# A transformer block with experts on one Trainium2 core: new beats of the first stage and a new order within the slots of the second attention

## The reference

```python
x = x + xattn0(layernorm(x), ctx)   # 16 heads of 8: cross attention, then self attention, then a Gelu FFN of 512,
                                    # each with projection, residual and layer norm
x = x + ffn0(layernorm(x))          # router top-2 of 8 experts with capacity (SiLU, inner 512) + shared expert (SiLU, 1024)
x = x + xattn1(layernorm(x), ctx)   # one head of 128, both directions, linear interpolation 77 -> 128, sigmoid gate
x = x + ffn1(layernorm(x))          # 8 experts, each takes its 33 best tokens of 128; h = gelu(tokens @ w1 + b1) @ w2 + b2
```

## Time and profile before

| | us |
|---|---|
| median of 3 runs | 1101.03 |
| lowest, highest | 1100.28, 1107.3 |
| the profiled execution | 1104.57 |
| its span in the profile | 1102.8 |
| eight beats without an FFN in it, starts of `s2` at 105.40 and 124.45 | 19.05 |

### The profile page before, as it was taken

How to read it: one execution, slowest core, us unless ns; L and a number is a source line. 1 busy time by engine, 2 the same in 40 slices (tenths; PEclk the granted TensorE clock), 3 DMA queues, 4 the chain that set the end, 5 groups by cost and what they waited for, 6 DMA issues and landing times.

```text
span 1102.8 us, 23340 instructions
## 1 busy us (share of the span) xinstructions
PE 978.3 (89%) x8694; PEld 766.7 (70%) x8694; DVE 651.8 (59%) x2135; ACT 585.8 (53%) x1341; POOL 466.7 (42%) x752
## 2 busy tenths in 40 slices
PE   4888898988888789899989999979978998989998
PEld 2556665656566567788878887857766876778877
DVE  4658865767576864756763333657786466455331
ACT  4668887786767677423333332333334653654453
POOL 6236645658585845666620000234455245113010
PEclk8889998897989899999999999988999998998999
DMA  7745442323232202000011332300001332321421
GB/s 182 184 122 152 113 118 69 85 64 84 82 82 77 76 18 83 13 14 6 4 37 53 106 105 56 105 20 20 20 20 18 99 87 25 82 77 38 137 61 55
DMA packets 72944, 78.58 MB, mean 71 GB/s; under 512 B 8469, under 2 KB 64132, under 8 KB 72832
## 3 DMA queue, kind: packets, MB, share of 16 engines
q1 hardware_dynamic: 67104, 69.61, 22.9%
q0 software_dynamic: 4096, 6.84, 2.9%
q10 hardware_dynamic: 1632, 0.64, 0.3%
HBM read 38.25 MB, written 11.68 MB: 45 GB/s over the span
## 4 chain that ended last, share of the span: by engine, by line
PE 55%; DVE 16%; ACT 11%; POOL 8%; issue 5%; DMA 3%; SPq 1%; DVEq 0%; POOLq 0%; ACTq 0%
PE pb L1075 5%; PE pb L1065 4%; PE pb L802 4%; PE pb L902 3%; PE pb L889 3%; PE pb L891 3%; DVE arena L1211 3%; PE pb L759 3%; PE pb L648 3%; PE pb L793 3%; PE pb L794 2%; DVE XB L1173 2%; PE pb L751 2%; DMA arena<-arena 2%; ACT arena L1685 2%
## 5 line engine op out<-in xcount | busy, mean ns | idle before, releaser
L1211 DVE TENSOR_REDUCE arena<-pb 128x4 f32<-128x308 f32 (+1 forms) x256 | 136.2, 575 | 64.5 <-PE pb L615 64.5
L1685 ACT ACTIVATE arena<-pb 77x512 f32<-77x512 f32 (+1 forms) x256 | 138.8, 597 | 54.3 <-PE pb L631 54.1
L2128 POOL DMA_INDIRECT arena<-yd,arena x64 | 63.5, 993 | 140.4 <-issue 140.4
L1740 ACT ACTIVATE arena<-pb 128x256 f32<-128x256 f32 x128 | 48.7, 385 | 131.2 <-PE pb L794 124.1
L1968 POOL TENSOR_SCALAR arena<-arena 128x4 f32<-128x4 f32 x48 | 9.4, 195 | 193.1 <-DVE arena L1166 191.4
L648 PE MATMUL pb<-arena 77*32 77x128 f32 (+1 forms) x2048 | 88.4, 294 | 0.0
L793 PE MATMUL pb<-XLT,arena 128*128 128x256 f32 x256 | 78.7, 389 | 1.2 <-DVE arena L1371 1.1
L794 PE MATMUL pb<-XLT,arena 128*128 128x256 f32 x256 | 77.3, 384 | 0.0
L2047 POOL DMA_INDIRECT xd<-XB,arena x64 | 64.0, 1000 | 29.4 <-issue 18.8
L1906 ACT ACTIVATE arena<-pb,arena 128x264 f32<-128x264 f32 x128 | 54.6, 484 | 40.7 <-PE pb L1065 40.6
L615 PEld LDWEIGHTS pb<-arena 64*128 64x128 bf16 x1024 | 29.4, 100 | 65.3 <-DVE arena L1211 28.7
(11 more groups left out here) (231 smaller groups left out, 2401.1 us busy)
## 6 DMA issues: line engine op xcount, KB each, us to landing
arena<-arena SPq DMA_DIRECT2D x190, 128.0 KB, 2.5
arena<-in_pe SPq DMA_DIRECT2D x32, 514.5 KB, 3.6
arena<-in_pr SPq DMA_DIRECT2D x8, 768.0 KB, 4.9
arena<-arena SPq DMA_DIRECT2D x43, 77.0 KB, 2.2
xd<-arena SPq DMA_DIRECT2D x8, 320.0 KB, 3.2
arena<-xd SPq DMA_DIRECT2D x8, 320.0 KB, 5.5
yd<-arena SPq DMA_DIRECT2D x8, 320.0 KB, 5.1
XO<-in_x SPq DMA_DIRECT2D x8, 256.0 KB, 3.6
```

The costliest lines, as they stand in the source:

```text
L1211: e.tensor_reduce(NM[i % 2][0][:, b, 4 * h:4 * h + 4, h2], bk[B + h2][:, 0:4 * nk].rearrange("p (t k) -> p t k", t=4), AX, ALU.max, negate ...
L1685: e.activation(PT[n % 2][0:nk, 512 * hf:512 * hf + 512], bk[2 + hf][0:nk, :], ACT.Exp, scale=SC8).then_inc(a_exp, 1)
L2128: e.indirect_dma_start(G[x % 8], None, yd, bass.IndirectOffsetOnAxis(ap=IDG.bitcast(U32)[:, k, b:b + 1], axis=0), bounds_check=None, oob_i ...
```

## The change

1. `exp` is one ACTIVATE over two neighbouring banks (1024 wide) instead of two of 512; `maxima` is one reduction over two banks. The semaphores count once a beat.
2. All four `ffn1` and Gelus of a group are in beat d = 20. Between the second and third product stand `s1`, the router and others.
3. Many calls of the first stage get another distance or another place within the beat, on every engine: s1 before the router's and FFN's products, `values` a beat later (d = -14), DVE's copy of the maxima's row before the layer-norm output, `rest` and `rest_mid` up to a beat earlier. In the early four "s" units (`hi=12`) the second statistics of the FFN norm are at d = 27 (before 26) and POOL's scale at 26 (before 27), POOL's first at 23 (24) and DVE's output at 25 (24); in the last four (`lo=12`) the first statistics are at 22 (23) and the second scale at 25 (27).
4. In the second attention the calls keep their slot or move by one, and stand in another order within it. Scores, maxima, exponentials and normalisation of the two directions are calls of their own (`x_scores(g, j)` at 8 and 9, `x_exp(g, j)` at 9 and 11, `x_norm(g, j)` at 10 and 11). `x_out` becomes `x_cross` and `x_self`, at 15. `lin kc` on ACT is at 8 (7), `val vc` on PE at 7 (6). Experts' steps `gather`, `oh`, `og`, `xe`, `ot` move by one step, `back`, `place` and `ys` come one earlier.

The core of the diff (helpers: `at(n, d, kinds, lo, hi)` gives the unit i with n - 8i = d):

```diff
             for n in range(BEAT0, BEAT1):
-                if 0 <= n < NCH:
-                    s2(n)
-                if 0 <= n - 1 < NCH:
-                    pv(n - 1)
...
+                for m in chunk_at(n, 0):
+                    s2(m)
+                for i, b in block_at(n, 5, "s"):
+                    two(i, b)
...
+                for m in chunk_at(n, 1):
+                    pv(m)
...
+                for i in at(n, 36, "s", hi=12):
+                    cum(group(i))
...
+                for i in at(n, 20, "s", hi=12):
+                    ffn1(group(i), 0)
...
+                for i in at(n, 20, "s", hi=12):
+                    ffn1(group(i), 1)
...
+                for m in chunk_at(n, -11):
+                    s1(m)
...
+                for i in at(n, 21, "s", hi=12):
+                    ffn2(group(i))
...
+                for i in at(n, 20, "s", hi=12):
+                    ffn1(group(i), 2)
...
+                for i in at(n, 28, "s", hi=12):
+                    t2(group(i))
...
-                for h2 in range(2):
-                    e.tensor_reduce(NM[i % 2][0][:, b, 4 * h:4 * h + 4, h2],
-                                    bk[B + h2][:, 0:4 * nk].rearrange("p (t k) -> p t k", t=4), AX, ALU.max,
-                                    negate=True).then_inc(v_max, 1)
+                sc = bk2[B // 2].rearrange("p (h x) -> p h x", h=2)[:, :, 0:4 * nk].rearrange("p h (t k) -> p h t k", t=4)
+                e.tensor_reduce(NM[i % 2][0][:, b, 4 * h:4 * h + 4, :].rearrange("p t h -> p h t"), sc, AX, ALU.max,
+                                negate=True).then_inc(v_max, 1)
...
+                for i in at(n, 27, "s", hi=12):
+                    L.wait_ge(g_f1, group(i) + 1)
+                    ln_stats(LNF, 2 * group(i) + 1, grp(XO, group(i)))
...
-                for hf in range(2):
-                    L.wait_ge(p_s2, n + 1)
-                    e.activation(PT[n % 2][0:nk, 512 * hf:512 * hf + 512], bk[2 + hf][0:nk, :], ACT.Exp,
-                                 scale=SC8).then_inc(a_exp, 1)
+                L.wait_ge(p_s2, n + 1)
+                e.activation(PT[n % 2][0:nk, :], bk2[1][0:nk, :], ACT.Exp, scale=SC8).then_inc(a_exp, 1)
...
-                        if d in (18, 20):
-                            gelu(g, d - 18)
-                            gelu(g, d - 17)
...
+                for i in at(n, 20, "s", hi=12):
+                    gelu(group(i), 0)
...
+                for i in at(n, 26, "s", hi=12):
+                    ln_scale_shift(LNF, 2 * group(i) + 1)
+                for i in at(n, 25, "s", lo=12):
+                    ln_scale_shift(LNF, 2 * group(i) + 1)
+                for i in at(n, -14, lo=2):
+                    rest_mid(2 * i + 1, (a_mid, 2 * i + 2), (g_rest, rests(i, 1)), g_rest, 512)
...
-                    if d == 10:
-                        x_exp(g)
...
+                for g in group_at(t, 9):
+                    x_exp(g, 0)
+                for g in group_at(t, 11):
+                    x_exp(g, 1)
```

939 lines of the change are left out of this document (514 added, 425 removed).

## The result

| | before | after |
|---|---|---|
| median of 20 runs each | 1106.76 | 1101.20 |
| lowest, highest | 1100.28, 1113.81 | 1087.26, 1105.52 |
| profiled execution, its span | 1104.57, 1102.8 | 1092.47, 1090.7 |

The ratio is 0.9935, 95% interval 0.9913 to 0.9956: 7 us less. Forecast were 29 less, range 1053 to 1097; the time lies outside it. Two later comparisons of the same kernel gave 0.9957 (0.9931 to 0.9984) and 0.9956 (0.9918 to 0.9994), so 5 to 7 us.

What follows compares the result with a forecast made beforehand. PE, busy 89%, was taken as the engine to feed, with short waits for others and lost clock. Terms 16 + 4 + 3 + 2 + 4 = 29 us less gave a forecast median of 1073, range 1053 to 1097.

Steps and rivals of the forecast that it cites:

- New beats of the rest, first stage: First stage's other moved calls: 3 us from the maxima's row, 0 from the router's chain, 2 from the last four units.
- the router's chain: First stage, FFN to router through DVE, POOL, ACT, PE: nothing won or lost, 0, bounds -1 and +2.4 us a unit.
- signs of being wrong: Router's-turn wait above 3 us, POOL idle before second scale, more half speed at 190-400 us, attention Gelu waits over 1 us.
- Four Gelus in a beat: First stage: twelve fewer table loads, both remaining loads under PE's work; 2.7 us a unit, 16 us, bounds 4 and 22.
- One exponential and one maximum: ACT and DVE, each beat: two-bank instructions cut 16 us of work; 4 us gained, bounds 0 and 16.
- The maxima's row: First stage: DVE's copy before the layer-norm output starts its DMA a microsecond earlier; 3 us, bounds 0 and 4.1.
- 251 for the statistics again: First stage, router's chain: DVE's FFN-norm statistics done at 251 us in the new order, against 251.07 in the trace before.
- The last four units: End of first stage: chain a beat earlier, PE's one wait of 3.0 us shrinks; 2 us, bounds 0 and 3.
- Second attention: Second attention: 2 us from normalised rows a slot earlier, 2 from shorter Gelu waits, 0 for added loads; 4 us.
- Eaten by the round: Rival, 190 to 400 us: lost ACT slack stops DVE and POOL, a third of 29 left; 1092, chance 0.23.
- The router's chain: As a rival: the early units' router chain becomes the bound, 10 us a unit, 41 in all; 1113, slower, chance 0.09.
- the rival: Clock rival: shorter waits leave fewer half-speed stretches, 12 us more in the first stage, some 7 in attention; 1054, chance 0.13.

Runs made afterwards that it cites:

- choice_same: Changed kernel with DVE's top-2 choice and selection of the early four groups one beat earlier, all else as changed; 1081.12 us, ratio 0.9790.
- gelu_only: Kernel before with only the four FFN products and Gelus of a group moved together to distance 20; 1101.18 us, ratio 0.9961.
- wide_only: Kernel before with only the exponential and the maximum over two banks, order untouched; 1094.75 us, ratio 0.9925.
- stage2_new: Kernel before with all edits of the second attention, first stage as before; 1112.01 us, ratio 0.9893.

## Why the prediction was wrong

**What failed** is the step "New beats of the rest, first stage". It went through the chain of the FFN's norm and the maxima's row, and priced the moves of DVE's `choose` and `select` and of POOL's `bias_norm` and `bias_ffn` at nothing, without naming what they would stand beside. They meet: 14 us of waits, 18.6 us of time. A second step of the same term failed too: the router's chain, put at 0, cost 5.8 to 7 us (below). Without the stands the sum looks close, since `choice_same` is 22.5 us below before and forecast were 29, but part of that is luck: by the traces its first stage is 13.6 us shorter where 25 were forecast, and the second attention gave 10 to 12 where 4 were. I looked at each engine's order against its semaphores, and two engines that share no semaphore there held each other up. The bounds did not cover it either: no term of the first stage had a loss of more than 2.4 us a unit, and the three stretches lost 6.7, 5.4 and 5.6. Of the signs of being wrong that were named, two came: more half speed between 190 and 400 us, and POOL idle before the second scale (0.29 us, at 240.47). PE's wait for the exponential, which was to fall below 2 us, fell to 5.2.

**Four Gelus in a beat** (16 forecast, bounds 4 to 22): the walk through the four beats held, the term did not. In the timelines of after, ACT and PE around the Gelus of beat 68, four beats from 66 to 70 took 16.1 us (209.41 to 225.50), as worked out:

```profile
215.70 1.28 ACT L1808 ACT_TABLE_LOAD   x1
216.99 1.27 ACT L1808 ACTIVATE arena<-pb,arena 128x512 f32<-128x512 f32 x2
...
220.34 1.64 ACT L1754 ACTIVATE XB<-XO,arena 128x128 f32<-128x128 f32 x4
221.99 1.28 ACT L1763 ACT_TABLE_LOAD   x1
223.29 1.02 ACT L1763 ACTIVATE arena<-pb 128x1024 f32<-128x1024 f32 x1
```

```profile
214.94 2.25 PE L773 MATMUL pb<-XLT,arena 128*128 128x512 f32 x4
...
217.73 1.98 PE L773 MATMUL pb<-XLT,arena 128*128 128x512 f32 x4 [0.30 <-ACT arena L1808]
...
221.73 3.84 PE L781 MATMUL pb<-arena 128*128 128x128 f32 x32
225.50 0.40 PE L653 MATMUL pb<-arena 64*128 64x128 bf16 x8
```

The second load lies under the long product, and ACT then waits for PE. The five stretches with Gelus are 16.3 us shorter in `choice_same`, but with the new order and both merges together. The Gelus alone (`gelu_only`) took 10.6 out of the five and added 1.1 to the sixth unit: some 9.5 of 16 by that trace, and 4 by its ratio. The 0.5 us for bank 6 came in one of six places (0.44, near 340 us); near 163 and 434 us PE waits 1.03 and 1.04 us for a Gelu instead, where below 0.5 was forecast, and beats 120 to 127 are 2.4 longer.

**One exponential and one maximum** (4, bounds 0 and 16): 4.9 us in the first stage by the trace of `wide_only`, 8 in all by its ratio. Held within its bounds. One working was not right: "the same overlap" of 0.12 us would make the pair of maxima 1.24 us, not 1.27, though 1.26 to 1.28 is what the pair takes in the trace of before.

**The maxima's row** (3): beats 0 to 47 are 5.9 us shorter, while neither merge alone shortens them, so it is the new order. No wait of `s2` for a DMA is left from 105 to 410 us, where 4.1 us stood. In beats 0 to 47 that wait went from 1.5 us to nothing, and the waits for maxima from 4.0 to 0.7; which of the moved calls did it was not tried apart.

**The router's chain** (0, bounds -1 and +2.4 a unit): it cost 1.4 us a stretch (105.6 to 111.4 over four, or 112.6 in `choice_same`, 1.75 each). PE's wait at the turn rose from 1.5 to 2.5, and ahead of it `s2` waits 1.2 for an exponential that stands on ACT behind a wait for POOL's remainder. My "251 for the statistics again" was the error. Against the start of `s2` in beat 75 they ended 0.8 us behind it in before (250.24 and 251.07), and 2.6 us behind it in after (237.8 and 240.39). POOL began its scale within 0.1 us of them, so DVE's statistics set the time, not POOL. The cost was inside the bounds, the value 0 was not right.

**The last four units** (2): the wait of 3.0 us is gone, and stretch 112 is shorter once nothing stands, but beats 120 to 127 lose 2.4. Not gained.

**Second attention** (4): 10 to 12 us (`stage2_new`, ratio 0.9893). PE's waits from 687 us on, for the router's turn in before, then from 690 us on for the same turn and for the Gelus in after (before: last line of the earlier trace rows):

```profile
PE pb L670 <- DVE XB L1173: 15.8, 5, 4.4
```

```profile
PE pb L692 <- DVE XB L1231: 7.7, 4, 4.4
...
PE pb L1118 <- ACT arena L2013: 3.2, 4, 0.9
```

The Gelu waits fell by 4.2, from 7.4 to 3.2 (2 forecast). What I had said to stay, the turns for the expert router, was halved: PE waited 4.28 us there at 825.30 in before and 1.11 at 827.17 in after, and of 2.36 and 2.71 at 907 and 991 us nothing and 0.34 are left; 2.2 and 1.6 us came at the turn of the counts (`ps`) ahead of it. DVE's order there is the same, as I had said, and its output only 1 us earlier (904.64 for 905.73). I had not asked what PE does meanwhile: `back` and `place` come a step earlier and now stand ahead of the turn.

**The rivals.** "Eaten by the round" had the nearest number, 1092, but its reason (ACT, DVE, POOL at 70%, many small stops) is not what happened: three long ones did it. "The router's chain" was right in place and small in size, 1.4 to 1.8 us a unit where it needed 7.2. The clock did not rise: 0.84 instead of 0.88 from 190 to 400 us. By the granted clock in the traces, half speed behind the Gelus of these 210 us is gone, as the rival had it (three stretches of 3.4 us before, none after). But three of 6.8, 3.4 and 6.8 us came beside or behind the stands, and those at the router's turns are 13.7, 13.7, 13.7 and 10.2 us long, where they were 10.2, 13.7, 10.2 and 6.8. So the two steps that failed cost a second time by the clock.

## What to carry to other kernels

When calls are moved, look beside DVE and POOL even where no semaphore joins them: small DVE instructions on SBUF data that come just ahead of a gapless run of POOL's tensor operations can take as long as the run. Look for rows whose longest is many times their median; the profile books it as busy. If the order cannot be changed, let POOL wait for its own last operation between them: 0.1 us each bought 10 to 12 us here. And test a large reordering part by part: one good and one bad part had nearly cancelled, and the good one was worth 22 us.
